# Computing the experts on tokens sorted by expert, gathered and scattered with indexed DMAs

## What is computed

```python
gate_weights = jax.nn.softmax(jnp.einsum('bld,de->ble', x, gate_W) + gate_b, axis=-1)
topk_vals, topk_idx = jax.lax.top_k(gate_weights, TOP_K)      # TOP_K = 2, E = 8
boost = x
for i in range(TOP_K):
    # _experts_all: h = relu(x W1 + b1), then h W2 + b2, for all 8 experts; the one-hot picks one
    eo = _selected_expert(boost, topk_idx[:, :, i], W1, b1, W2, b2)
    outs.append(eo)
    if i < TOP_K - 1:
        boost = boost + ALPHA * eo                             # ALPHA = 0.5
fused = sum(topk_vals[:, :, i:i + 1] * outs[i] for i in range(TOP_K))
return _layer_norm(residual + fused, ln_gamma, ln_beta)
```

## Time and profile before

| | us |
|---|---|
| Median of 3 runs | 2937.82 |
| Lowest, highest | 2935.97, 2939.99 |
| The profiled execution, its own time | 2918.93 |
| Its span, first to last instruction | 2917.1 |
| Mean granted clock of TensorE | 0.966 of full |
| Busy share PE, DVE, ACT, POOL | 89%, 86%, 81%, 48% |
| Experts stage (fence to fence) | 269.2 |

### The profile page before, as it was taken

The page is one execution under the profiler, slowest core; times in us unless marked ns, Lnnn a source line. Parts: engine busy times, 40 slices in busy tenths (PEclk is TensorE's granted clock), DMA queues, the critical chain, the costliest instruction groups (busy, mean ns, idle before and its releaser), DMA issues.

```text
span 2917.1 us, 78807 instructions
## 1 busy us (share of the span) xinstructions
PE 2585.8 (89%) x30925; PEld 1342.9 (46%) x30925; DVE 2520.8 (86%) x3657; ACT 2354.9 (81%) x4175; POOL 1388.4 (48%) x2752
## 2 busy tenths in 40 slices
PE   6877799978999999999999999999999999999856
PEld 3444477743444444444444444444444444444335
DVE  4888735379999999999999999999999999999966
ACT  5887433459999899999999999899998999998832
POOL 3443421112566445665446654456644566444564
PEclk8888799989999999999999999999999999999978
DMA  2000000422222123221231212313123222220000
GB/s 63 1 1 1 16 1 1 71 46 45 35 39 38 25 45 54 36 41 23 45 58 32 45 29 35 60 30 45 33 31 61 34 40 36 27 45 10 2 1 15
DMA packets 86770, 94.44 MB, mean 32 GB/s; under 512 B 4592, under 2 KB 84736, under 8 KB 85632
## 3 DMA queue, kind: packets, MB, share of 16 engines
q1 hardware_dynamic: 86400, 89.41, 18.8%
HBM read 69.47 MB, written 19.92 MB: 31 GB/s over the span
## 4 chain that ended last, share of the span: by engine, by line
PE 43%; DVE 20%; issue 15%; POOL 12%; ACT 10%; DVEq 0%; POOLq 0%; DMA 0%; ACTq 0%
DVE NM L1295 13%; PE bank L719 9%; PE bank L730 9%; ACT E L986 5%; PE bank L663 4%; PE bank L645 4%; PE bank L635 4%; PE bank L675 3%; PE bank L682 3%; POOL acc L1495 3%; PE bank L555 2%; PE bank L572 2%; ACT dBT L889 1%; POOL smp L1488 1%; DVE hs L1116 1%
## 5 line engine op out<-in xcount | busy, mean ns | idle before, releaser
L1295 DVE TENSOR_REDUCE NM<-bank 128x1 f32<-128x1024 f32 x1536 | 1803.6, 1207 | 98.3 <-PE bank L719 83.1
L986 ACT ACTIVATE E<-bank,NM 128x1024 f32<-128x1024 f32 x1536 | 1708.2, 1116 | 197.8 <-DVE NM L1295 125.9
L719 PE MATMUL bank<-KS,QS 128*32 128x512 bf16 x12288 | 950.8, 383 | 140.3 <-ACT E L986 94.0
L730 PE MATMUL bank<-E,dg 128*32 128x256 f32 x12288 | 920.6, 382 | 3.4 <-issue 1.7
L1554 POOL TENSOR_TENSOR dg<-mask,RZ 128x128 f32<-128x128 f32 x384 | 153.3, 399 | 895.6 <-DVE RZ L1305 891.4
L719 PEld LDWEIGHTS bank<-KS,QS 128*32 128x32 bf16 x12288 | 258.7, 95 | 662.8 <-ACT E L986 519.1
L730 PEld LDWEIGHTS bank<-E,dg 128*32 128x32 f32 x12288 | 355.2, 109 | 331.2 <-issue 96.5
L986 ACT ACTIVATION_READ_ACCUMULATOR E<-bank,NM 128x1 f32 x1536 | 306.9, 200 | 0.0
L1495 POOL TENSOR_TENSOR acc<-acc,rel 128x256 f32<-128x256 f32 x384 | 272.7, 731 | 10.6 <-ACT acc L948 10.6
L663 PE MATMUL bank<-H,ET 128*128 128x129 f32 x1536 | 198.9, 282 | 6.2 <-DVE ET L1236 6.2
L663 PEld LDWEIGHTS bank<-H,ET 128*128 128x128 f32 x1536 | 180.4, 192 | 47.1 <-issue 37.3
(11 more groups left out here) (230 smaller groups left out, 2837.5 us busy)
## 6 DMA issues: line engine op xcount, KB each, us to landing
KS<-scratch SPq DMA_DIRECT2D x216, 128.0 KB
QS<-scratch SPq DMA_DIRECT2D x216, 128.0 KB
scratch<-UB SPq DMA_DIRECT2D x24, 768.0 KB, 3.7
WL<-in_wl SPq DMA_DIRECT2D x6, 1091.0 KB, 19.0
X<-in_x SPq DMA_DIRECT2D x4, 256.0 KB, 6.9
W<-in_moe_w SPq DMA_DIRECT2D x1, 1024.0 KB, 9.0
out<-X SPq DMA_DIRECT2D x8, 128.0 KB, 1.8
rel<-in_rel SPq DMA_DIRECT2D x1, 960.0 KB, 5.0
```

The costliest lines, as they stand in the source:

```text
L719: inst = PE_.matmul(bank[x % 3][32 * i:32 * i + 32, k * 512:k * 512 + 512], QS[:, half % 2, 4 * hq + i, r0:r0 + 32], KS[:, b, 4 * hq + i, ...
L730: inst = PE_.matmul(pb(6)[32 * k:32 * k + 32, 256 * grp:256 * grp + 256], dg[:, x // 4 % 3, x % 4, :], E[:, x % NE, :].rearrange("p (i k c ...
L986: A_.activation(E[:, x % NE, :], bank[x % 3][:, :], ACT.Exp, bias=NM[:, x % 4:x % 4 + 1], accum_out=ZS[:, quad % 3, j:j + 1]).then_inc(s[" ...
L1295: V.tensor_reduce(NM[:, x % 4:x % 4 + 1], bank[x % 3][:, :], AX.X, ALU.max, negate=True).then_inc(s["rowmax"], 1)
```

## The change

Tokens are sorted by expert, and each tile of 128 rows is computed by one expert only.

- **Sorting.** DVE makes signed one-hots (OHS) and running sums (SUM); PE multiplies them by a triangular matrix and by ones (rank_pe), which counts for each token how many of its expert came before. From that DVE takes each token's row in a sorted tensor, for both passes (place_dve). Experts in pairs fill a region from both ends. units_dve derives a table of the 23 tiles of each pass: its expert (EXPERT) and its first row (FIRSTROW). 23 is the number of tiles that suffices for every input.
- **Scatter.** POOL writes the 16 tiles of token records (REC: 128 numbers, the row of the second pass, the token's number, two weights; 528 bytes) to their rows in DRAM with 16 indirect DMAs. Beforehand SP fills both sorted tensors (6.2 MB each) with spare records, during the scan.
- **Units.** Per pass 23 units. SP loads the table entry into a register and with it the unit's 128 rows (rows_of) and its expert's W1 and b1 (weights, a ring of four, 129 KB each). PE transposes the tile (L610), ACT copies it, PE computes the up product (L618, two matmuls of 128 columns), ACT applies ReLU, PE loads the expert's number into a register and computes the down product and bias (L629, L630, three matmuls of 128 columns). DVE forms the second pass's input (L1271), or the weighted sum (L1273, L1274). POOL scatters the tile, in the first pass to the second sorted tensor, in the second to a tensor in token order (mixed).
- **Order of the passes.** SP loads no row of a pass before all scatters ahead of it have landed. SP's program is: four weight sets, 23 row loads, the next weight sets up to that of unit 26, 23 row loads, the rest of the weights, then four loads of the result (Y).
- **Moved.** The gating of chunks 1 and 2 goes from beside the units to the end of the scan (GATES, positions 129 to 139), that of chunk 3 behind the fence. All weighted sums, norms, projections and splits come after the last unit; the second half of batch 0 is split by DVE (L1279 to L1282) into buffers of its own (PQ1, QF1). The zeroing of QS and KS and the load of the first layer's weights are DMAs from ACT's queue at the stage's start.
- **Removed.** GATE, AFTER, beside, the 64 units, the bias products and the transposes for the second pass. Several semaphores share a name with others now (ld_rows, made, early, ld_moe), with counts adjusted.

```diff
-GATES0 = {"PE": {106: "etr", 108: "egate", 116: "eot"},
...
-          "DVE": {100: "bn0", 103: "n0", 109: "gl", 112: "top"},
-          "POOL": {100: "pow0"}}
...
+         "DVE": {100: (0, "bn0"), 103: (0, "n0"), 109: (0, "gl"), 112: (0, "top"), 129: (1, "bn0"), 130: (2, "bn0"), 131: (1, "n0"),
+                 133: (2, "n0"), 136: (1, "gl"), 137: (2, "gl"), 138: (1, "top"), 139: (2, "top")},
+         "POOL": {100: (0, "pow0"), 129: (1, "pow0"), 130: (2, "pow0")}}
...
+UNITS, WIDE, SPAN = 23, 132, 17 * 128
+ROWS = UNITS * 128 + 4 * SPAN
...
+        def units_pe(e, i):
+            for u in range(UNITS + 2):
+                if u < UNITS:
+                    n = UNITS * i + u
+                    e.wait_ge(s[f"ld_rows{n % 6}"], loads_before(n) + 16)
...
+                    PE_.transpose(pb(n % 2)[:, 0:128], UT_[:, u, 0:128], ident[:, :]).then_inc(s["unit_tr"], 1)
+                if 0 <= u - 1 < UNITS:
+                    n = UNITS * i + u - 1
+                    e.wait_ge(s[f"ld_w{n % 4}"], 16 * (n // 4) + 16)
+                    e.wait_ge(s["unit_rt"], n + 1)
...
+                    for hc in range(2):
+                        inst = PE_.matmul(pb(2 + n % 2)[:, hc * 128:hc * 128 + 128], WS[:, n % 4, hc * 128:hc * 128 + 128],
+                                          RT2[:, n % 2, :], start=True, stop=True)
+                    inst.then_inc(s["unit_up"], 1)
+                if u >= 2:
+                    n = UNITS * i + u - 2
+                    ex = e.value_load(EXPERT[0:1, i, u - 2:u - 1], min_val=0, max_val=7)
+                    e.wait_ge(s["unit_hs"], n + 1)
...
+                    for hc in range(2):
+                        PE_.matmul(o, HS[:, n % 3, hc, :], W2[:, bass.ds(ex, 1), hc, :].rearrange("p e h -> p (e h)"), start=(hc == 0), stop=False)
+                    PE_.matmul(o, mc_("first"), b2[:, bass.ds(ex, 1), :].rearrange("p e h -> p (e h)"), start=False, stop=True).then_inc(s["unit_dn"], 1)
...
+            for j in range(4):
+                e.wait_ge(s["place"], j + 1)
+                for i in range(4 * j, 4 * j + 4):
+                    G.indirect_dma_start(io["sorted"][0][:, :], bass.IndirectOffsetOnAxis(ap=POS[:, i:i + 1], axis=0), REC[:, i, :], None).then_inc(s["scattered"], 16)
...
+            for i in range(2):
+                for u in range(UNITS):
+                    e.wait_ge(s["unit_out"], UNITS * i + u + 1)
+                    at = bass.IndirectOffsetOnAxis(ap=UT_[:, u, 128 + i:129 + i].bitcast(mybir.dt.uint32), axis=0)
...
+            def weights(n):
+                if n >= 4:
+                    e.wait_ge(s["unit_hs"], n - 3)
+                ex = e.value_load(EXPERT[0:1, n // UNITS, n % UNITS:n % UNITS + 1], min_val=0, max_val=7)
+                e.dma_start(WS[:, n % 4, :], io["moe_w1"][bass.ds(ex, 1), :, :].rearrange("e p w -> (e p) w")).then_inc(s[f"ld_w{n % 4}"], 16)
+
+            def rows_of(i):
+                e.wait_ge(s["scattered"], 16 * (NT + UNITS * i))
+                for u in range(UNITS):
...
+                    row = e.value_load(FIRSTROW[0:1, i, u:u + 1], min_val=0, max_val=ROWS - 128)
+                    e.dma_start(UT_[:, u, :], io["sorted"][i][bass.ds(row, 128), :]).then_inc(s[f"ld_rows{n % 6}"], 16)
+
+            for n in range(4):
+                weights(n)
+            rows_of(0)
+            for n in range(4, UNITS + 4):
+                weights(n)
+            rows_of(1)
+            for n in range(UNITS + 4, 2 * UNITS):
+                weights(n)
+            e.wait_ge(s["scattered"], 16 * (NT + 2 * UNITS))
+            for j in range(4):
+                e.dma_start(Y[:, tiles(j), :], io["mixed"][j * CH:j * CH + CH, :].rearrange("(n p) d -> p n d", p=128)).then_inc(s[f"ld_rows{j}"], 16)
```

490 lines of the change are left out of this document (275 added, 215 removed).

## The result

The changed kernel is faster: a median of 2908.2 us in four runs (2904.9 to 2909.7) against 2938.6 us of the kernel before in the same series, a ratio of 0.990 [0.988, 0.991]. Two further series of it, on two chips, gave 0.993 [0.992, 0.995] (2918.6 us, six runs) and 0.995 [0.993, 0.997] (2920.7 us, twelve runs). So the gain is some 16 to 30 us, 0.5 to 1.0%, where the prediction had a loss of 42 us and gave the faster side 12%. Rival (1) had named 2909 us; the time is that of the first series, the stage is not (see the end).

What follows compares the result with a forecast made beforehand. PE was taken to bound the experts stage only. Scan end 11, fence to rows 33.6, rounds 171.9, tail 93 and low clock 2 gave 311.5 us against 269.2, +42, so 2980 us forecast, range 2920 to 3065.

Steps and rivals of the forecast that it cites:

- Rival (1): Whole stage: register loads and POOL cheap, clock stays high; stage 240 us, 2909 us in all; chance 0.12.
- p: Time per unit in a round's second part, set by PE at a partly low clock: 2.4 us.
- S: End of the scan, which gains norms and gates of chunks 1 and 2: +11 us, floor 6, ceiling 15.
- F: From the fence to the first row load, with table, scatters and their landing: 33.6 us.
- x: POOL's time per indirect DMA among the 16 first scatters: 1.3 us.
- R: One round of 23 units, from row loads to the last scatter's landing: 85.3 us.
- t: SP's time per row load, with register load, register instructions and DMA issue: 1.3 us.
- 2R: Both rounds of units, with 1.3 us for the second round's first issue: 171.9 us.
- Z: From the last scatter landed to the attention, all now waiting in a row: 93 us, where before had 12.
- Low clock at the attention's start: Attention's start: PE comes out of an idle stretch at a low clock, costing 2 us.
- (2): SP and PE: register loads dear at 1.3 us, stage 358 us, 3027 us in all; chance 0.14.
- (3): Scatters: POOL is the bound at 3.0 us each, stage 365 us, 3034 us in all; chance 0.13.

Runs made afterwards that it cites:

- both: Changed kernel with all first-layer weight sets loaded once and copied per unit by DVE, zeros written by ACT itself: 2866.3 us, ratio 0.975.
- zeros_act: Changed kernel with ACT writing the zeros of QS and KS itself in twelve activations instead of three DMAs: 2913.0 us beside 2918.6.
- pe_no_load: Version both with PE taking expert n mod 8 without a register load, so the output is of other experts: 2871.8 us, ratio 0.979.
- rows_static: Changed kernel with the 46 first rows written as constants, so SP loads no register for a row load: 2889.5 us, ratio 0.985.
- after_look: Changed kernel unedited, one more look on the same chip as two looks at the kernel before: that run took 2905.0 us.
- pool_twice: Changed kernel with a second indirect DMA on POOL for each unit of the first round: 2949.4 us.

## Why the prediction was wrong

**The structure was right, and one term was mis-sized: p, the time of a unit, 2.4 us where 1.42 was measured.** Predicted against measured, in the changed kernel's first trace:

- **S**, +11: measured +7.8, and +9.1 as a mean of four. Right in kind; L1080, the scan's last instruction on DVE, starts at 362.29 behind the top-2 chains of chunks 1 and 2.
- **F**, 33.6: measured 41.2. x = 1.3 was right (0.96 busy and 0.30 between). POOL's first scatter starts 9.9 us behind the fence and not 8. The landing was the miss: 3.5 us behind the last scatter, taken from mb's lone load, where 10.3 us were measured (11.2 from the scatter's start). I had listed the zeros as removed from POOL and forgot that the change puts them on ACT's queue at the same moment. Without them the landing takes at most 2.6 us from the start (both). Of the 7.6 us the edit of zeros_act gives back 4.5 before SP's weight sets are late.
- **R**, 85.3 a round: measured 61.5 and 61.3. This is the step that failed. Of the 23.9 us, 19 x (2.4 - 1.42) = 18.6 are p and 28.6 - 24.8 = 3.8 are t. The text had the right number in hand: 1.25 us of pure PE work at full clock, which pe_no_load shows as 1.22 to 1.24. It was raised to 2.4 for two reasons, and both were wrong. The clock: "a PE that waits 29 us per round will not be held at the high clock" is true of the first units only. The windows of the first round's second part:

```profile
430.20:433.00 2.80, 0.59 (x3) 0.59 (x3) 0.00 (x0) 0.00 (x0) 0.00 (x0) 0.50 0.42 116
433.00:436.00 3.00, 3.00 (x17) 3.00 (x17) 0.29 (x1) 0.97 (x4) 0.48 (x1) 0.55 0.39 96
436.00:439.00 3.00, 3.00 (x29) 2.99 (x28) 0.58 (x2) 2.36 (x8) 2.00 (x3) 1.00 0.42 123
442.00:462.00 20.00, 19.46 (x149) 17.48 (x147) 4.08 (x14) 11.47 (x38) 13.11 (x15) 1.00 0.54 141
```

  The granted clock is 0.50 and 0.55 (1.2 GHz) until 436 us and 1.00 (2.4 GHz) behind it, for all but the first units. The register load: 0.8 us was assumed "partly beside" the products; 0.2 of it is what PE pays (1.42 against 1.22, pe_no_load). On SP, where nothing hides it, it costs 0.65 (rows_static).
- **2R** instead of 171.9: 122.8, 49 us less. In the two traces with the lumps it is 133 and 134 us, in after_look 122.
- **Z**, 93: measured 86.4 (33.4 from Y's load to the store, 53.0 from there to the first scores). It rested on rows for every item and was within 7 us, 3 in each half.
- **Low clock at the attention's start**, +2: worth nothing. The kernel before starts its attention at the low clock too (granted 0.50 from 624.9 to 630.0), and from the first reduction on the two first traces have 2291.0 and 2291.5 us.

The sum with measured terms is 7.8 + 41.2 + 122.8 + 86.4 = 258.2 against 269.2, 11 us faster, as the traces of the two first runs say. The attention, priced at no change, gave 9 us more in the mean of four traces, though nothing in the two first ones; that step was wrong by an effect that no row of the one trace at hand showed. The step from the trace to the median, +19 for both kernels, was wrong in the same way: the profiled run of the kernel before was a lucky one, 19 us under its median, and the changed kernel's first was at its own series' median. With 19 us on both sides the 11 us of the traces would have made 2927; the first series came out at 2908 by the attention and by what stays open above.

**The rivals.** (1) had p = 1.5 and t = 0.7; p was right, t was 1.13, R 61.4 and not 53.6, F 41.2 and not 28.5. Its stage of 240 us was 18 short of the measured 258.2, and that its 2909 us met the first median is luck. Its break-even at R = 66 came out too low: the two traces with rounds of 66 to 68 us reach the attention's first reduction at 619.0 and 619.5 us, the four of the kernel before at 622.8 to 626.1. (2) fell with pe_no_load, where PE's part of a load is 0.2; on SP a load is 0.65. (3) fell with x = 1.26, but its mechanism is real: pool_twice shows that at 2.5 us a unit POOL sets the round.
The range began at 2920, where two later medians were 2918.6 and 2920.7. It left out most of (1), though its p was the one value that the rows themselves gave.

## What to carry to other kernels

Size a new stage from the pure work that rows give, and raise it only for something that is waited for: a register load cost 0.65 us on SP, which issues DMAs by it, and 0.2 on PE under queued products, and a clock that had fallen in an idle stretch was back within the first few units, so the low level was a price for these and not for the stage. Count every transfer that the change starts in the same window as a latency on the path; here 6.3 MB of zeros made 3 us into 11. And doubling a cost tells what a second one costs; only leaving it out tells what the first one does, and even that only between units that nothing else holds up.

## What the runs showed of the hardware

- An indirect DMA of 128 rows of 528 bytes occupies POOL for 0.96 us, and the next follows 0.30 us later. The last one of the second round landed 2.25 us behind its start. The Trainium skill ("DMA: Bandwidth & Descriptors", Anatomy of one DMA) fits a DMA issued by GpSimd at 2.0 us and its bytes over 436 GB/s, 2.15 us for such a tile. The trace agrees with that as the time to the landing; as an occupancy of POOL it would be too much.
- Indirect DMAs beside a chain of short handoffs can make it lumpy: 1.26, 1.26, 2.5 us instead of a steady 1.42, and with POOL at its limit (pool_twice) PE stands for 2.5 to 4.7 us at a time. In two of four traces of the same program the lumps were absent.
- A register load that PE needs for the addresses of its products took 0.2 of 1.42 us a unit under queued products, and a second one right behind it 0.64.
- A last indirect write landed 11.2 us behind its start with 6.3 MB of loads queued beside it, and within 2.6 us without them.
- A kernel can have stalls of 2 us in PE at fixed places of the program that another version of it, with the same code there, doesn't have.
